# Pre-norm decoder layer: ScalarE normalises the cross-attention tokens, expert lows on GpSimd, last self-attention scores ahead of two cross projections

## The reference, cut to what matters

```python
x = x + _L0_attn_ref(_layernorm(x, axis=-1), ...)                    # 16 heads of 64, no mask
x = x + _L0_xattn_ref(_layernorm(x, axis=-1), ctx_1024, ctx_1024, mask_1x1xSxS2_bk0, ...)  # 16 heads of 16
x = x + _L0_ffn_ref(_layernorm(x, axis=-1), ...)                     # 8 experts 256 -> 512 -> 256, all computed,
                                                                     # their sum times one gate value per token
...
m = jnp.mean(x, axis=axis, keepdims=True)
v = jnp.var(x, axis=axis, keepdims=True)
return (x - m) / jnp.sqrt(v + eps)
```

## Time and profile before

| | us |
|---|---|
| median of 3 runs (855.07 to 857.67) | 855.11 |
| the profiled execution's own time | 854.01 |
| its span, first to last instruction | 852.2 |
| PE busy in it | 817.1 |
| DVE, ACT, POOL busy in it | 447.7, 476.8, 227.4 |

### The profile page before, as it was taken

How to read it: one execution, slowest core, us unless ns; L and a number is a source line. 1 busy time by engine, 2 the same in 40 slices (tenths; PEclk the granted TensorE clock), 3 DMA queues, 4 the chain that set the end, 5 groups by cost and what they waited for, 6 DMA issues and landing times.

```text
span 852.2 us, 16891 instructions
## 1 busy us (share of the span) xinstructions
PE 817.1 (96%) x6171; PEld 711.1 (83%) x6171; DVE 447.7 (53%) x935; ACT 476.8 (56%) x1532; POOL 227.4 (27%) x221
## 2 busy tenths in 40 slices
PE   9999999999999987999887999999999999999998
PEld 7778888888888875777775899999999899999997
DVE  4564664564555548899988554552233322433223
ACT  5555555455464546777777467544544454444543
POOL 3443343123233444668575400000000000000000
PEclk9999999999999999999998999999999999999999
DMA  6311000000000065666471233100000000000000
GB/s 193 108 51 39 1 2 2 2 1 2 2 25 2 2 151 146 167 144 179 99 195 51 62 100 99 50 26 2 1 1 2 25 0 0 0 25 1 1 1 25
DMA packets 22889, 42.22 MB, mean 50 GB/s; under 512 B 3352, under 2 KB 3872, under 8 KB 22816
## 3 DMA queue, kind: packets, MB, share of 16 engines
q1 hardware_dynamic: 21936, 40.64, 17.6%
q10 hardware_dynamic: 880, 0.60, 0.3%
HBM read 30.35 MB, written 10.49 MB: 48 GB/s over the span
## 4 chain that ended last, share of the span: by engine, by line
PE 81%; DVE 9%; DMA 3%; issue 3%; ACT 2%; POOL 2%; SPq 0%; POOLq 0%; ACTq 0%; DVEq 0%
PE Y L720 27%; PE A L720 25%; PE S L720 11%; PE T L847 5%; PE S L838 3%; PE O L881 3%; ACT probs L1127 2%; DMA arena<-stage 2%; DVE probs L1300 1%; DVE nm L1291 1%; PE S L819 1%; DVE xn L1231 1%; DMA stage<-arena 1%; PE O L868 1%; PE S L949 1%
## 5 line engine op out<-in xcount | busy, mean ns | idle before, releaser
L1127 ACT ACTIVATE probs<-S,nm 128x128 f32<-128x128 f32 x512 | 180.5, 378 | 127.3 <-DVE nm L1291 127.2
L720 PEld LDWEIGHTS Y<-arena,PT 128*128 128x128 f32 x1536 | 199.9, 191 | 11.4 <-DVE PT L1203 1.4
L1203 DVE TENSOR_TENSOR PT<-probs,PT 128x512 fp32r<-128x512 f32 x128 | 89.7, 702 | 227.5 <-ACT PT L1183 227.5
L720 PE MATMUL Y<-arena,PT 128*128 128x256 f32 x1536 | 203.8, 283 | 0.4
L1551 POOL TENSOR_TENSOR probs<-probs,rinv 128x512 f32<-128x512 f32 x128 | 134.3, 1049 | 236.3 <-DVE rinv L1296 236.3
L720 PE MATMUL A<-XT,arena 128*128 128x512 f32 x612 | 159.2, 394 | 0.0
L1183 ACT ACTIVATE PT<-probs 128x512 fp32r<-128x512 f32 x128 | 80.8, 631 | 106.9 <-PE Y L720 106.5
L1300 DVE COPY probs<-T 128x512 f32<-128x512 f32 x96 | 66.0, 688 | 113.3 <-PE T L847 112.9
L720 PEld LDWEIGHTS A<-XT,arena 128*128 128x128 f32 x612 | 108.1, 189 | 17.9
L1127 ACT ACTIVATION_READ_ACCUMULATOR probs<-S,nm 128x1 f32 x512 | 111.2, 217 | 0.0
L720 PE MATMUL S<-XT,arena 128*128 128x512 f32 x384 | 99.7, 395 | 0.0
(11 more groups left out here) (124 smaller groups left out, 996.4 us busy)
## 6 DMA issues: line engine op xcount, KB each, us to landing
wst<-in_pieces SPq DMA_DIRECT2D x43, 256.0 KB, 2.6
stage<-arena SPq DMA_DIRECT2D x32, 256.0 KB, 2.8
arena<-stage SPq DMA_DIRECT2D x51, 128.0 KB, 3.9
arena<-stage SPq DMA_DIRECT2D x21, 256.0 KB, 3.9
craw<-in_ctxT SPq DMA_DIRECT2D x4, 512.0 KB, 4.1
out<-craw SPq DMA_DIRECT2D x8, 256.0 KB, 2.0
xs<-in_x SPq DMA_DIRECT2D x3, 512.0 KB, 5.4
craw<-in_pieces SPq DMA_DIRECT2D x6, 256.0 KB, 2.6
```

The costliest lines, as they stand in the source:

```text
L720: mm = pe.matmul(acc, lhs[a], rhs[b], start=first and i == 0, stop=last and i == 2, skip_group_check=shared)
L1127: last = act.activation(probs[:, ring(ph, g, n), u * P:(u + 1) * P], S[n % 2][:, u * P:(u + 1) * P], ACT.Exp, bias=nm[:, n % 4, u:u + 1], ...
L1203: dve.tensor_tensor(out_, src, hi.bitcast(F32), ALU.subtract).then_inc(sem_, 1)
```

## The change

Four edits. (1) Last quads of self-attention: the projections 2 and 3 of slot 9 move behind that slot's scores, product and output projection, the V projections move from slots 10 and 11 to 12 and 13, and POOL blanks the key area before it splits the next context. (2) For groups 1 to 3 of phase 1 and group 0 of phase 2, VectorE writes only `shift` = -mean x rstd, and ScalarE writes `xn` = rstd x `xs` + `shift` behind the exponentials of the same slots. (3) The residual of cross-attention groups 0 to 2 is added in two halves, in slots 7 and 8, in place of both in slot 7. (4) The lows of the first six experts go to GpSimd, in slots 4, 6, 7, 9, 13 and 14.

```diff
-        V1 = ({SKIP + 6: [(0, BOTH)], SKIP + 7: [(1, BOTH)]},
+        V1 = ({SKIP + 8: [(0, BOTH)], SKIP + 9: [(1, BOTH)]},
...
+        def shifted(ph, g):
+
+            return ph == 1 and g > 0 or ph == 2 and opening(g)
...
-                    if ph == 0 and g == GROUPS - 1:
+                    if (g == GROUPS - 1) == (ph == 0):
                         half = v - SCORES[ph] - at
                         return [((half,),)] if half in BOTH else []
...
-                    return [(g + 1, part) for part in {10: (0, 1, 2), 15: (3,)}.get(v, ())]
+                    return [(g + 1, part) for part in {12: (0, 1, 2), 15: (3,)}.get(v, ())]
...
-                    kind = 3 if n - skip > MIXED[0] else 4 if n - skip == MIXED[0] else 0
+                    kind = 3 if n - skip > MIXED[0] else {5: 6, 6: 7, 7: 4}.get(n - skip, 0)
...
+        FIRST_LOWS = (4, 6, 7, 9, 13, 14)
...
+            (("transpose", "odd", (1, 0)), ("scores", "even", (0, 0)), ("pv", "odd", (1, 0)),
+             ("proj", "proj", (3, 6)), ("qk", "qk", (0, 0))),
+            (("transpose", "even", (1, 0)), ("proj", "proj", (3, 6))))
...
-            (("probs", "odd", (1, 0)), ("out", "odd", (1, 0)), ("out_low", "odd", (1, 0)),
-             ("max", "cross", (0, 0)), ("stats", "stats", (0, 0))),
+            (("probs", "odd", (1, 0)), ("out", "odd", (1, 0)), ("max", "cross", (0, 0)),
+             ("out_low", "odd", (1, 0)), ("stats", "stats", (0, 0))),
...
+            def normalise(ph, g, tiles):
+
+                if not shifted(ph, g):
+                    return
+                act.wait_ge(ln_shift, g if ph == 1 else GROUPS)
+                if ph == 1 and g == 1:
+                    act.wait_ge(xp_ps, xpe(1, 0, 3))
+                else:
+                    act.wait_ge(xt_ps, xte(ph, g, -1))
+                for t in tiles:
+                    last = act.activation(xn[:, t, :], xs[:, g * TILES + t, :], ACT.Identity,
+                                          bias=shift[:, t:t + 1], scale=rstd[:, t:t + 1])
+                if tiles[-1] == TILES - 1:
+                    last.then_inc(ln_x, 1)
...
+                if shifted(ph, g):
+                    if tiles[0] == 0:
+                        dve.scalar_tensor_tensor(shift[:, :], mv[:, :, 0], -1.0, rstd[:, :], ALU.mult,
+                                                 ALU.mult).then_inc(ln_shift, 1)
+                    return
...
-                if ph == 2 and n in FIRST_EXPERTS:
-                    expert_lo(FIRST_EXPERTS.index(n))
...
+            def expert_low(m):
+
+                at = m * 2 * PIECE
+                pool.wait_ge(e_hi, m + 1)
+                pool.tensor_tensor(arena[:, at + PIECE:at + 2 * PIECE], raw_expert(m),
+                                   arena[:, at:at + PIECE].bitcast(F32), ALU.subtract).then_inc(e_split, 1)
+
             def once(ph, g, n):
+                if ph == 2 and n in FIRST_LOWS:
+                    expert_low(FIRST_LOWS.index(n))
```

More of the change, by code:

```diff
@@ L184, in build @@
         rstd = sb("rstd", [P, TILES], F32)
+        shift = sb("shift", [P, TILES], F32)
         lg = sb("lg", [P, 5, TILES * EXPERTS], F32)
@@ L255, in build @@
         ln_rstd = sem("ln_rstd")
+        ln_shift = sem("ln_shift")
         ln_x = sem("ln_x")
@@ L355, in steps @@
             if name in ("qk_out", "v_out"):
-                behind = ph == 1 and not opening(g) or ph == 0 and opening(g) and v < SCORES[0]
+                behind = ph == 1 and not (opening(g) and v == SKIP + 4) or ph == 0 and opening(g) and v < SCORES[0]
+                if ph == 1 and opening(g) and v == SKIP + 5:
+                    return []
                 return [(j,) for j, halves in steps(name.split("_")[0], ph, g, v - behind) if 1 in halves]
@@ L520, in build @@
              ("transpose", "cross", (0, 3)), ("v", "v", (0, 0)), ("qk", "qk", (0, 0))),
-            (("transpose", "odd", (1, 0)), ("proj", "proj", (3, 6)), ("v", "v", (0, 0)),
+            (("transpose", "odd", (1, 0)), ("proj", "proj", (3, 6)),
              ("pv", "odd", (1, 0)), ("scores", "cross", (0, 0))),
-            (("scores", "even", (0, 0)), ("v", "v", (0, 0)), ("qk", "qk", (0, 0))))
+            (("scores", "even", (0, 0)), ("v", "v", (0, 0)), ("qk", "qk", (0, 0))),
+            (("transpose", "odd", (1, 0)), ("scores", "even", (0, 0)), ("pv", "odd", (1, 0)),
+             ("proj", "proj", (3, 6)), ("qk", "qk", (0, 0))),
+            (("transpose", "even", (1, 0)), ("proj", "proj", (3, 6))))
         ACT_ORDER = (
@@ L565, in build @@
              ("ctx", "ctx", (0, 0))),
-            (("normalise", "quad", (1, 2)), ("blank", "blank", (0, 0)), ("out_hi", "cross", (0, 5)),
-             ("out_low", "cross", (0, 6)), ("ctx", "ctx", (0, 0))))
+            (("normalise", "quad", (1, 2)), ("blank", "blank", (0, 0))),
+            (("normalise", "quad", (1, 2)),),
+            (("normalise", "quad", (1, 2)),),
+            (("normalise", "quad", (1, 2)),))
         block = ctx.enter_context(nc.Block())
@@ L1220, in ln_apply @@
             def ln_apply(ph, g, tiles):
-                dve.wait_ge(ln_rstd, nth(GRP, ph, g, 0))
-                if ph == 0 and g > 1 or ph == 1 and g < 2:
-                    dve.wait_ge(xp_ps, xpe(ph, g, -1) if parted(ph, g) else xpe(1, 0, 3))
+                if tiles[0] == 0:
+                    dve.wait_ge(ln_rstd, nth(GRP, ph, g, 0))
+                if shifted(ph, g):
+                    if tiles[0] == 0:
+                        dve.scalar_tensor_tensor(shift[:, :], mv[:, :, 0], -1.0, rstd[:, :], ALU.mult,
+                                                 ALU.mult).then_inc(ln_shift, 1)
+                    return
+                if ph == 0 and g > 1 or ph == 1:
+                    dve.wait_ge(xp_ps, xpe(ph, g, -1))
                 elif not (ph == 0 and g == 0):
@@ L1486, in experts @@
                     if isinstance(g, int) and g == 0 and m + LEAD < MCH:
+                        if m == 0:
+                            dve.wait_ge(e_split, LEAD)
                         expert_lo(m + LEAD)
```

14 lines of the change are left out of this document (10 added, 4 removed), and 1 row of the table ACT_ORDER.

## The result

The changed kernel takes 850.84 us in the median of 8 runs (848.97 to 853.46), against 856.84 for the kernel before in as many: a ratio of 0.9929 (95% interval 0.9903 to 0.9955), or 6.1 us less. The forecast was 844.0 in 840.8 to 849.6. The direction was right; of the 11.1 us about half came, and the median lies outside the range. The forecast also started from 855.11, the median of three runs of before, where eight give 856.84: 1.7 of the 6.8 us between 844.0 and 850.84 have nothing to do with the change. One run of all reported here, of e12, took 1123.56 us at a granted clock of 0.653 and is left out.

A forecast was written before the change was run, and what follows sets the result against it. PE was taken to bound the kernel, so only its waits and half-clock stretches could give time back. Terms summed to -11.1: 854.01 became 842.9, plus 1.1 from profiled run to median gave 844.0 us, 80% in 840.8 to 849.6.

The forecast's parts named there:

- the 11.1 us: Whole kernel: the summed gain, -4.8 - 2.8 - 2.2 + 0 - 3.0 + 1.7 = -11.1 us.
- the three places: PE's waits lie where self-attention meets cross-attention, twice in each cross-attention group, and in the last cross-attention tail.
- Edit 1, at its place: Meeting of self- and cross-attention: group 1's key projection starts at 326.6 against 331.38, -4.8 us.
- later staging: After the meeting: staging from `stack_queries` waits for the last `Y`, which comes equally earlier; costed at nothing.
- what PE saves stays saved: Whole kernel: PE's savings ahead of 482 us remain, as no PE wait of size follows.
- each gain is swallowed by the next staging transfer: Rival for the whole kernel: no change, 855.1 us; chance 3%.
- its -2.8 and -2.2: `xn` on ScalarE: 2.8 us back at the borders of groups 2 and 3, 2.2 at the last.
- the row for `shift`: Group borders: DVE loses four `xn` and gets one 128x4 instruction, some 0.1 us.
- The price of `xn`: ScalarE at the group borders: 0.36 us from start to start for each `xn`.
- a rule that the prediction used elsewhere: Tail lows: a DVE instruction with two SBUF inputs blocks against a GpSimd one reading SBUF; POOL's lows stay at 1.28.
- Edit 3: Residual by halves in cross-attention: removes a 0.74 us wait, but the next query transfer's wait grows to 1.18; 0.
- The net forecast there: Last cross-attention tail: lows on GpSimd give -3.0 us, one clock fall of 3.4 us takes back +1.7.

The follow-up runs named there:

- e12: e7 with the meeting of self-attention and cross-attention ordered as in the kernel before; 846.95 us, ratio 0.9913 to the kernel before.
- e5: e4 plus 30 semaphore-count instructions among TensorE's warm-up products, to move an instruction fetch forward; 847.19 us, ratio 0.9900 to the kernel before.
- e6: e4 plus 140 semaphore-count instructions among TensorE's warm-up products, to move an instruction fetch forward; 862.63 us, ratio 1.0078 to the kernel before.
- e10: e9 plus 44 semaphore-count instructions among 16 TensorE warm-up products instead of 20 products without them; 842.72 us, ratio 0.9861 to the kernel before.
- e2: Changed kernel with VectorE again normalising all tokens, the other edits kept; 849.71 us, ratio 0.9942 to the kernel before.
- e7: Changed kernel with `shift` alone one slot earlier for groups 2 and 3 and the last border; 845.92 us, ratio 0.9883 to the kernel before.
- e4: Changed kernel with `shift` and `xn` both one slot earlier for groups 2 and 3 and the last border; 846.63 us, ratio 0.9899 to the kernel before.
- e8: e4 with the residual of groups 0 to 2 added whole in one slot again; 845.53 us, ratio 0.9892 to the kernel before.
- e1: Changed kernel with only the re-ordered meeting of self-attention and cross-attention kept, other edits undone; 853.12 us, ratio 0.9967 to the kernel before.
- e9: e7 with the fourth expert's low on GpSimd in slot 11 of the tail instead of 9; 842.31 us, ratio 0.9848 to the kernel before.
- e11: The changed kernel run again unaltered, on another chip; 850.04 us, ratio 0.9942 to the kernel before.

## Why the prediction was wrong

**What bounds the kernel**: right, and the three places were the right ones. What was not seen is a fourth, the transfer wait ahead of group 1's first scores, since it was 1.08 us in before, and the third fall of the clock in before, at 331.8.

**Edit 1, at its place**: right. Both transposes' waits went, the first scores wait for `kq_first` (0.31, where 1.3 was taken: with the lead of 0.95 from before the meeting put back on, PE was ready at 313.1 and not 312.2, and the transfer was there at 313.4, where 313.5 was taken), the `Y` waits 0.97 for the low of `AT` (0.75 was taken), and the key projection came at 325.33; with the 0.95, 326.3 against the forecast's 326.6.

**Edit 1, what lies behind**: this step failed. The prediction costed later staging at nothing, and held that what PE saves stays saved. Under the rival "each gain is swallowed by the next staging transfer" it argued that those chains start from PE's own projections and move along. They do start 5.0 us earlier, and 2.7 us of that is lost by group 1's first scores. Of the chain of transfers there, the key staging grew from 2.8 to 4.3 us; e5, e6 and e10 show that this part comes from the fetch of TensorE's instructions, which did not move up with it. Taking it away gave back 0.9 of the wait in e5 and in e10. The rest of the 2.7 was not isolated. In the traces it lies in the query staging, which grew from 3.3 (346.75 to 350.04) to 5.4 (341.76 to 347.18), and 0.6 in the query stack. The query staging is issued 8.0 us behind the key staging in both kernels, since it waits for VectorE, so a long key staging doesn't delay its issue. But it stands behind the key stack in the queue. The last transfer of that stack lands 1.8 us past the issue of the query staging in before (issued at 343.73, 4.8 to landing) and 3.6 past it now (340.29 and 5.1). In e10 that is 2.2, and the query staging still takes 4.9, with a fetch of 886 ns at 344.7 in it; whether that one is the cause stays open. The rival got 3%; what happened was half of it, a mix with the forecast that had no case of its own.

**Edit 2**: its -2.8 and -2.2 were mis-sized as made; they came to about nothing (e2). The step that failed is the row for `shift`, "some 0.1 us", together with "it waits for `shift`, behind which the exponentials queue". The wait was named and not priced: `shift` takes 0.54 to 0.93 us and stands last on DVE in its slot, so ScalarE stood 1.5 us with the exponentials behind it. The price of `xn` was also short (0.60 alone and 1.09 for two, 0.49 from start to start, for 0.36), but e7 shows that it doesn't matter: with `shift` a slot earlier edit 2 is worth some 3 to 5 us (e4, e7), where the forecast has 5.0.

The row above also answers to a rule that the prediction used elsewhere. `shift` of 128x4 takes 0.82 us where a reciprocal of that size takes 0.17 in the same stretch, and it ends with POOL's L1641, at 366.6. In the Trainium skill, SBUF — State Buffer (Who interferes with whom) says that a DVE instruction with two SBUF inputs contends with a GpSimd instruction that reads SBUF. By that rule the trace agrees: `shift` is such an instruction, and all four end 0.02 us behind a GpSimd instruction. I had it at hand for the lows and did not put it to the one instruction that the edit adds to DVE.

**Edit 3**: right, 0 (e8). Its place shows 0.65 by halves where the whole took 0.74.

**Edit 4 and the clock**: the lows took 1.27 to 1.28 us as forecast, and the waits were for POOL (1.7 us) and ScalarE. From the tail's first transposes (451.64 to 450.92) to its last (474.83 to 471.11) the lead grows by 3.0. The net forecast there was 1.3, with a fall of the clock charged to the tail; in the profiled run the falls came at the meeting and behind the transfer wait instead, and cost there what was saved here. This is the third step that failed: the sum has the half clock of before go from 10.2 us to 3.4, and in the two profiled runs it is 13.6 in both.

**The sum** by what was shown, against -11.1: edit 1 some -2.8 (e1), edit 2 nothing, edit 4 -1.0 by the times or -2.1 beside the other edits (e1 to e2): -4 to -5, where two sets measured -6.1 and -5.0. With the intervals of the single runs that is no contradiction, and no exact account either.

## What to carry to other kernels

When a step moves from one in-order engine to another, price the small result that it now hands over: where it stands in the giver's queue, and what the taker has queued behind the wait. Here one 128x4 instruction a slot too late cost all of a gain of some 4 us. And when a stretch of work moves forward by some microseconds, everything that does not move with it, such as the fetch of instructions, meets other transfers; look in the trace at what lies on the DMA engines at the new time, not only at what lay there before.

## What the runs showed of the hardware that was not expected

- A fetch of 16384 B of instructions for TensorE held one of 16 DMA engines for 0.95 us in a gap (before, 335.9) and for 1.28 to 1.62 us beside the key staging (the changed kernel, e1, e2, e4, e7, e8, e9, e11). The staging then landed 1.5 us later (4.3 for 2.8), with the other engines done.
- A DVE instruction of 128x4 with two inputs in SBUF took 0.54 to 0.93 us beside POOL, and each of the four ended 0.02 us behind the POOL instruction; a 128x4 reciprocal, with one input, took 0.17 us beside POOL's L1591.
- An instruction on TensorE that only counts up a semaphore cost 0.10 us, behind a warm-up product too (e6: 7 of them make 0.32 us from product to product 1.05).
- ScalarE's activation with scale and shift by partition, 128x256 from SBUF to SBUF, took 0.60 us, against 0.40 for the copy of that size out of PSUM.
